# Second attention: exponentials per head out of PSUM, shares divided before they are turned, no matmuls with ones

## What is computed

```python
q = (x @ Wq + bq).reshape(B, N, NUM_HEADS, HEAD_DIM)
k = (y @ Wk + bk).reshape(B, M, NUM_HEADS, HEAD_DIM)
v = (y @ Wv + bv).reshape(B, M, NUM_HEADS, HEAD_DIM)
scale = 1.0 / np.sqrt(HEAD_DIM)
scores = jnp.einsum('bnhd,bmhd->bhnm', q, k) * scale
attn = jax.nn.softmax(scores, axis=-1)
out = jnp.einsum('bhnm,bmhd->bnhd', attn, v).reshape(B, N, IMAGE_DIM)
h = jax.nn.relu(out @ W1 + b1)
return h @ W2 + b2
```

## Time and profile before

| | |
|---|---|
| median of three runs | 781.83 us (780.53 to 781.97) |
| span of the profiled execution | 779.1 us |
| busy: PE, PEld | 651.9 us (84%), 451.2 us (58%) |
| busy: DVE, ACT, POOL | 369.5 us (47%), 221.6 us (28%), 181.0 us (23%) |
| chain that ended last, by engine | PE 56%, issue 16%, DVE 8%, DMA 8%, ACT 5% |
| mean granted clock of PE | 0.937 of full speed |

### The profile page before, as it was taken

The page is one execution under the profiler, slowest core; times in us unless marked ns, Lnnn a source line. Parts: engine busy times, 40 slices in busy tenths (PEclk is TensorE's granted clock), DMA queues, the critical chain, the costliest instruction groups (busy, mean ns, idle before and its releaser), DMA issues.

```text
span 779.1 us, 10605 instructions
## 1 busy us (share of the span) xinstructions
PE 651.9 (84%) x3506; PEld 451.2 (58%) x3507; DVE 369.5 (47%) x925; ACT 221.6 (28%) x361; POOL 181.0 (23%) x151
## 2 busy tenths in 40 slices
PE   4968689998799988999978973198999989898993
PEld 3746457686477863768746752145555555555552
DVE  4443649638486384685536675622232222222221
ACT  1241254431455224454124410021221212121220
POOL 2100223002330013120022100413333333334332
PEclk9987799999999998999988995589999999999998
DMA  9900100002000011000070202012222222222222
GB/s 351 407 21 1 54 1 1 2 21 94 14 0 0 20 54 54 0 0 0 0 261 36 82 0 58 7 29 41 41 41 41 40 42 34 43 35 43 36 35 26
DMA packets 20756, 40.27 MB, mean 52 GB/s; under 512 B 3872, under 2 KB 17440, under 8 KB 19456
## 3 DMA queue, kind: packets, MB, share of 16 engines
q1 hardware_dynamic: 8736, 25.16, 8.6%
q0 software_dynamic: 7488, 10.39, 8.2%
q10 hardware_dynamic: 4512, 4.46, 1.7%
HBM read 30.37 MB, written 9.64 MB: 51 GB/s over the span
## 4 chain that ended last, share of the span: by engine, by line
PE 56%; issue 16%; DVE 8%; DMA 8%; ACT 5%; POOL 3%; DVEq 3%; POOLq 1%; ACTq 0%
PE ps L617 33%; PE ps L948 11%; PE ps L621 8%; DMA keep<-normed,row_in 6%; PE ps L963 4%; POOL var_xh L300 1%; ACT ring L482 1%; DVE mx L1127 1%; DMA out_x<-OT,row_out 1%; DVEq L1040 1%; ACT keep L586 1%; DVE ring L1131 1%; POOL ring L357 1%; DVE rc L1137 1%; DVE XH L1008 1%
## 5 line engine op out<-in xcount | busy, mean ns | idle before, releaser
L948 PE MATMUL ps<-experts,keep 128*128 x312 | 144.7, 607 | 8.1 <-ACT keep L586 7.8
L1404 DVE SCALAR_TENSOR_TENSOR keep<-keep,row_w,ps 128x512 f32<-128x512 f32 x39 | 29.2, 749 | 151.9 <-ACT keep L590 151.9
L948 PEld LDWEIGHTS ps<-experts,keep 128*128 128x128 f32 x312 | 56.9, 192 | 70.1 <-issue 69.7
L374 POOL DMA_INDIRECT out_x<-OT,row_out x39 | 61.8, 1584 | 147.9 <-DVE row_out L1412 86.6
L963 PE MATMUL ps<-experts,keep 128*128 x312 | 73.9, 380 | 2.0 <-DVE keep L1408 2.0
L300 POOL TENSOR_TENSOR var_xh<-var_xh,minus_half 128x4 f32<-128x4 f32 x16 | 16.9, 1059 | 250.4 <-DVE var_xh L1003 250.4
L617 PE MATMUL ps<-experts,keep 128*128 128x256 f32 (+1 forms) x184 | 70.1, 533 | 5.9 <-DVE experts L1067 2.8
L963 PEld LDWEIGHTS ps<-experts,keep 128*128 128x128 f32 x312 | 59.1, 190 | 26.2 <-issue 20.1
L617 PE MATMUL ps<-ring,V 128*32 128x128 f32 x512 | 64.3, 279 | 1.5 <-DVE OT L1139 1.5
L1127 DVE TENSOR_REDUCE mx<-ps 128x8 f32<-128x1024 f32 x32 | 39.1, 1220 | 53.8 <-PE ps L617 53.8
L617 PE MATMUL ps<-ring,keep 128*32 128x128 f32 x512 | 63.5, 273 | 0.0
(11 more groups left out here) (209 smaller groups left out, 942.9 us busy)
## 6 DMA issues: line engine op xcount, KB each, us to landing
experts<-in_experts SPq DMA_DIRECT2D x8, 1536.0 KB, 16.6
keep<-in_keep SPq DMA_DIRECT2D x1, 3075.0 KB, 19.1
ring<-in_fold SPq DMA_DIRECT2D x1, 2112.0 KB, 11.2
experts<-in_x SPq DMA_DIRECT2D x4, 512.0 KB, 3.5
experts<-in_ctxT SPq DMA_DIRECT2D x4, 512.0 KB, 4.1
out_x<-X ACTq DMA_DIRECT2D x4, 512.0 KB, 3.1
normed<-XH ACTq DMA_DIRECT2D x4, 512.0 KB, 4.0
experts<-in_ctx SPq DMA_DIRECT2D x4, 384.0 KB, 3.4
```

Source lines behind the costliest of these rows:

```text
L374: pool.indirect_dma_start(out=out_d, out_offset=bass.IndirectOffsetOnAxis(ap=row_out[u][:, 0:1], axis=0), in_=YO[u], in_offset=None, compu ...
L948: ins = pe.matmul(ps[:, 2 * u + g, :], XIT[u][:, k, :], experts[:, bass.ds(at + (2 * k + g) * INTER, INTER)], start=(k == 0), stop=(k == K ...
L1404: dve.scalar_tensor_tensor(HA[u], HA[u], row_w[u][:, 0:1], ps[:, 2 * u + 1, :], ALU.mult, ALU.mult).then_inc(act_ok, 1)
```

## The change

The softmax of the second attention is rearranged. `most1` takes the place of `shift`: DVE still finds the largest score of each head, and then makes of it minus the largest times the scale (128 x 8 values), and no longer subtracts. `exp1` becomes eight instructions, one for each head: ACT reads the 128 scores of the head from PSUM, with the bias of the head, writes `PP`, and accumulates their sum into one column of `den`. `share1` on DVE takes the reciprocal of the eight sums and multiplies all 1024 exponentials by it. Transposes, their copy and `attend1` follow; `attend1` has no matmuls with ones, and goes over the stripes first and over the two halves of the heads second, so that matmuls in a row write different stripes. `keep1` copies the result from PSUM to `OT`. The streams are ordered anew around it, and the scores' banks are given back by the exponentials instead of by the subtraction.

```diff
-            def exp1(n, u):
-                act.wait_ge(s["sub"], UNITS * n + u + 1)
-                act.activation(PP[u % 2], PP[u % 2], ACT.Exp, scale=float(HD) ** -0.5).then_inc(s["exp"], 1)
+            def exp1(n, u, at=3):
+                act.wait_ge(s["mx"], UNITS * n + u + 1)
+                if u >= 2:
+                    act.wait_ge(s["pt_ps"], UNITS * n + u - 1)
+                for h in range(HT8):
+                    ins = act.activation(PP[u % 2][:, h, :], bank(at + h // HT4)[:, h % HT4 * S:(h % HT4 + 1) * S], ACT.Exp,
+                                         bias=mx[u % 2][:, h:h + 1], scale=float(HD) ** -0.5, accum_out=den[u % 2][:, h:h + 1])
+                ins.then_inc(s["exp"], 1)
...
             query1(LAST)
             value1(LAST)
+            exp1(LAST, 0)
             for u in range(UNITS):
-                exp1(LAST, u)
+                if u + 1 < UNITS:
+                    exp1(LAST, u + 1, 0 if u % 2 == 0 else 3)
                 probs1_turned(LAST, u)
...
                 pe.wait_ge(s["kb"], UNITS * n + u + 1)
                 if u >= ahead:
-                    pe.wait_ge(s["sub"], UNITS * n + u + 1 - ahead)
+                    pe.wait_ge(s["exp"], UNITS * n + u + 1 - ahead)
...
             def turn_probs1(n, u):
-                pe.wait_ge(s["exp"], UNITS * n + u + 1)
+                pe.wait_ge(s["norm"], UNITS * n + u + 1)
...
-                for st in range(4):
-                    out = ps[32 * st:32 * st + 32, attend_bank(u), :]
-                    mm(out[:, 0:S], [(V1[:, bb, o, 32 * (4 * t + st):32 * (4 * t + st) + 32], PQ[u % 2][:, 2 * st + o, :]) for o in range(2)])
-                    ins = mm(out[:, S:2 * S], [(kept("ones_half", 2)[:, o, :], PQ[u % 2][:, 2 * st + o, :]) for o in range(2)])
+                for o in range(2):
+                    for st in range(4):
+                        ins = pe.matmul(ps[32 * st:32 * st + 32, attend_bank(u), 0:S], V1[:, bb, o, 32 * (4 * t + st):32 * (4 * t + st) + 32],
+                                        PQ[u % 2][:, 2 * st + o, :], start=(o == 0), stop=(o == 1))
...
-            def shift(n, u, at=3):
-                sc = ps[:, at:at + 2, :].rearrange("p t (h n) -> p (t h) n", h=4)
+            def most1(n, u, at=3):
                 dve.wait_ge(s["sc_ps"], UNITS * n + u + 1)
-                dve.tensor_reduce(mx[u % 2][:, :], sc, AXX, ALU.max)
-                settle()
-                if u >= 2:
-                    dve.wait_ge(s["pt_ps"], UNITS * n + u - 1)
-                dve.tensor_tensor(PP[u % 2], sc, mx[u % 2][:, :].unsqueeze(2).broadcast_to([P, HT8, S]), ALU.subtract).then_inc(s["sub"], 1)
-
-            def divide(n, u):
+                dve.tensor_reduce(mx[u % 2][:, :], ps[:, at:at + 2, :].rearrange("p t (h n) -> p (t h) n", h=4), AXX, ALU.max)
+                settle()
+                dve.tensor_scalar(mx[u % 2][:, :], mx[u % 2][:, :], -float(HD) ** -0.5, None, ALU.mult).then_inc(s["mx"], 1)
+
+            def share1(n, u):
+                dve.wait_ge(s["exp"], UNITS * n + u + 1)
+                dve.reciprocal(den[u % 2][:, :], den[u % 2][:, :])
+                settle()
+                dve.tensor_tensor(PP[u % 2], PP[u % 2], den[u % 2][:, :].unsqueeze(2).broadcast_to([P, HT8, S]), ALU.mult).then_inc(s["norm"], 1)
+
+            def keep1(n, u):
                 bb, t = u // 2, u % 2
                 dve.wait_ge(s["ot_ps"], UNITS * n + u + 1)
-                o = attend_bank(u)
-                dve.reciprocal(rc[u % 2][:, :], bank(o)[:, S:2 * S])
-                settle()
-                dve.tensor_tensor(OT[:, t, bb * S:(bb + 1) * S], bank(o)[:, 0:S], rc[u % 2][:, :], ALU.mult).then_inc(s["ot"], 1)
+                dve.tensor_copy(OT[:, t, bb * S:(bb + 1) * S], bank(attend_bank(u))[:, 0:S]).then_inc(s["ot"], 1)
...
-                divide(n, 3)
-                shift(n, 6)
-                divide(n, 4)
-                shift(n, 7)
+                for u in (4, 5, 6):
+                    share1(n, u)
+                    most1(n, u + 1)
+                    keep1(n, u - 1)
                 top(n + 1)
...
+            most1(LAST, 0)
             for u in range(UNITS):
-                shift(LAST, u, 0 if u % 2 else 3)
-                if u >= 2:
-                    divide(LAST, u - 2)
-            divide(LAST, UNITS - 2)
-            divide(LAST, UNITS - 1)
+                if u + 1 < UNITS:
+                    most1(LAST, u + 1, 0 if u % 2 == 0 else 3)
+                share1(LAST, u)
+                if u:
+                    keep1(LAST, u - 1)
+            keep1(LAST, UNITS - 1)
```

More of the change, by code:

```diff
@@ L163, in build @@
         mx = [sb(f"mx{n}", [P, HT8]) for n in range(2)]
-        rc = [sb(f"rc{n}", [P, P]) for n in range(2)]
+        den = [sb(f"den{n}", [P, HT8]) for n in range(2)]
         gl = sb("gl", [P, B, NE])
@@ L209, in build @@
                  "xh3 xb xT3_ps xT3 k_ps k v1_ps v1 q1_ps q1 f_ps f y_ps xh4 xT4_ps xT4 gl_ps gl "
-                 "kb sc_ps sub exp pt_ps pt ot_ps ot")
+                 "kb sc_ps mx exp norm pt_ps pt ot_ps ot")
         names += "".join(f" var_{m} rs_{m}" for m in norms)
@@ L541, in _ @@
                 query(n + 1)
+                exp1(n, 1)
                 probs1_turned(n, 0)
-                exp1(n, 1)
                 exp_scores(n + 1)
+                exp1(n, 2)
                 probs1_turned(n, 1)
@@ L548, in _ @@
                 for u in (2, 3, 4):
-                    exp1(n, u)
+                    exp1(n, u + 1)
                     probs1_turned(n, u)
                 rows2_turned(n + 1)
-                exp1(n, 5)
+                exp1(n, 6)
                 probs1_turned(n, 5)
                 hidden(n + 1)
-                exp1(n, 6)
+                exp1(n, 7)
                 probs1_turned(n, 6)
-                exp1(n, 7)
                 exp_logits(n + 1)
@@ L866, in _ @@
                 score1(n, 2)
+                attend1(n, 0)
                 turn_probs1(n, 1)
-                attend1(n, 0)
                 turn_probs(n + 1)
                 score1(n, 3)
+                attend1(n, 1)
                 attend(n + 1)
                 turn_probs1(n, 2)
-                attend1(n, 1)
                 score1(n, 4)
+                attend1(n, 2)
                 turn_probs1(n, 3)
-                attend1(n, 2)
                 score1(n, 5)
+                attend1(n, 3)
                 turn_probs1(n, 4)
                 turn_x2(n + 1)
-                attend1(n, 3)
                 score1(n, 6)
+                attend1(n, 4)
                 turn_probs1(n, 5)
-                attend1(n, 4)
                 hidden(n + 1)
                 score1(n, 7)
+                attend1(n, 5)
+                turn_probs1(n, 6)
                 logits(n + 1)
-                turn_probs1(n, 6)
-                attend1(n, 5)
+                attend1(n, 6)
                 turn_probs1(n, 7)
-                attend1(n, 6)
                 attend1(n, 7)
@@ L1271, in _ @@
                 norm_in(n + 1)
-                shift(n, 0)
-                shift(n, 1)
+                most1(n, 0)
+                share1(n, 0)
+                most1(n, 1)
                 most(n + 1)
-                shift(n, 2)
-                divide(n, 0)
+                share1(n, 1)
+                most1(n, 2)
+                keep1(n, 0)
                 over_sum(n + 1)
-                shift(n, 3)
+                share1(n, 2)
+                most1(n, 3)
+                keep1(n, 1)
                 add_attention(n + 1)
-                divide(n, 1)
                 gather_stats("xh2")
-                shift(n, 4)
+                share1(n, 3)
+                most1(n, 4)
+                keep1(n, 2)
                 norm(n + 1, X0, XH0, D, "xh2")
-                divide(n, 2)
-                shift(n, 5)
-                divide(n, 3)
-                shift(n, 6)
-                divide(n, 4)
-                shift(n, 7)
+                for u in (4, 5, 6):
+                    share1(n, u)
+                    most1(n, u + 1)
+                    keep1(n, u - 1)
                 top(n + 1)
-                divide(n, 5)
-                divide(n, 6)
-                divide(n, 7)
+                share1(n, 7)
+                keep1(n, 6)
+                keep1(n, 7)
                 shares(n + 1)
```

## The result

The kernel after takes 822.1 us in the median (819.5 to 826.8), the kernel before 781.87: a ratio of 1.0525 [1.049, 1.056], slower by 40 us.

The account below looks back on a forecast made before the run. PE bounds the kernel before; after the change, rings of waits and a falling clock. 1.8 + 9.3 + 8.7 + 10.5 = 30.3 us on the 779.1 us span gives 809.4, as median 812; range 790 to 829.

Parts of the forecast that it names:

- rival B: PE stays at half clock for nearly all of the attention: 50 us slower, 832 us; chance 0.13.
- rival D: `attend1` gains nothing by going abreast (2.4 us): 10 us more, 822; chance 0.56 together with the forecast.
- Behind the loop, the ring: Last attention: waits through PE, DVE and ACT make 6.15 us a unit instead of 4.47, +9.3 us.
- `attend1` at 0.95 us: Matmuls of `attend1` run two abreast, 0.95 us instead of 2.4; four abreast would be 0.5.
- The clock behind the loop, "half of it", 8.7: Last attention: half clock for five units and the tail costs 17.5 us; half counted, 8.7.
- The clock in the loop, 10.5: Loop trips: clock falls at the trip's end (3 us) and in the middle (0.5), 10.5 us in three trips.
- The loop's ring, +0.6 a trip: Loop: one pair of score banks makes 5.9 us a unit, a trip 0.6 us longer, 1.8 us in three.
- 0.17 for the small multiply: In `most1` on DVE, the small multiply behind the largest scores takes 0.17 us of 1.47.
- In the loop PE was at 1.00 throughout: Kernel before, loop: PE's granted clock was 1.00 throughout; falls were expected there after the change.
- Exponentials, 2.88 us a unit: ACT: eight per-head exponentials at 0.345 us each with the sum's read, 2.88 us with the last one's end.
- A (the clock holds, 793): Clock holds at 2.4 GHz where it did; only the two rings remain, 11 us slower, 793; chance 0.22.
- C (faster): Loop is bound by work, not its ring: 41 us instead of 52.1, in full 758 us; chance 0.09.

Follow-up runs that it names:

- after_warm: The kernel after plus matmuls nothing reads, added where PE idles behind the loop and in its trips; 795.7 us, 1.0174 of before.
- before_order: The kernel before with only the order of `attend1`'s matmuls changed, stripes in the inner loop, all sixteen kept; 755.6 us, 0.9668 of before.
- after_nosums: The kernel after with its eight exponentials a unit no longer accumulating their sums, shares left undivided; 804.5 us, 1.0307 of before.

## Why the prediction was right, and where it was off

The direction and the mechanism were right: PE has less to do, the rings take the place of its work, and the clock follows. The sum was short by 10 us (812 for 822), between the forecast and rival B. That 822 is also the number of rival D is chance, since what D supposes did not happen.

- **Behind the loop, the ring.** Forecast 6.15 us a unit at full clock and +9.3. after_warm shows 5.70, links in the order forecast, and +8.2 (49.7 against 41.6). The 0.45 less is mostly `attend1`. By the forecast's own scale a shorter `attend1` should have brought the +9.3 to some +6.5; the small multiply, held for 1.8 us in one unit (below), makes most of the difference.
- **`attend1` at 0.95 us.** Mis-sized: 0.57 at full clock, the fourfold case. The forecast took two abreast from the earlier trace rows; but no four matmuls in a row wrote four stripes there, so the rows could not show more. D (no gain) is refuted.
- **The clock behind the loop, "half of it", 8.7.** Measured 12.0. The whole attention at half would have been 17.5, and the stretch stood at 0.68: some two thirds of it, not half.
- **The clock in the loop, 10.5.** Measured 12.4 between the profiled executions of after and after_warm; 14.4 if all that the medians leave is put there. The falls come where they were expected, `hidden1` at 8.39 among them, and once more in mid-trip: scores of units 3 and 5 both take 2.08 in trip 2.
- **The loop's ring, +0.6 a trip.** This failed. Measured as the forecast did, from the first exponential to `hidden1`, it is 52.1 us in trips 1 and 2 of before (55.1 in trip 3, with its pause and half clock), 58.2 to 58.5 in after, and with the clock mostly held, in after_warm, 56.4, 55.7 and 55.7. So the ring costs 3.6 us a trip and more. The term that failed is "0.17 for the small multiply", taken without a look at what GpSimd does beside it: twice a trip, in units 0 and 5, it takes 1.7 to 2.1 us, and the second of these lies in the stretch of the forecast. In trip 2 of after_warm the starts of scores from unit 2 on are 5.7, 6.7, 8.1, 7.4 and 6.0 us apart, not 5.9. The 7.4 holds the multiply. The 8.1 is `add_attention`, which puts the product of unit 3 back (its exponentials end at 230.0, its reciprocal starts at 232.28) by 2.4 us in all where the forecast had 1.4. In the 6.7 the scores still run at half clock (2.08). Taking the multiply out (after_min) gives 3.1 to 3.9 us a stage, 15.5 in all, with the drain and the clock that go with it.
- **"In the loop PE was at 1.00 throughout".** That stretch is the first trip. The third trip of before fell to half clock (0.55 from 302.8 to 309.4 us), so a fall in the loop needs none of this change.
- **Exponentials, 2.88 us a unit.** Right (2.75 to 2.92). That the sums are the dear part of them, 27 us in the order of before, stood in no term, since the forecast priced the form as a whole.
- **A (the clock holds, 793).** after_warm nearly makes this case: 795.7. Its condition was wrong. Its size fits in part by luck: the ring of the loop is six times the 0.6 us a trip that it had, and the slow starts of trips 2 and 3 of before hide some of that.
- **C (faster).** The work that goes from PE is real, but 44 us of it (2.4 to 1.01 in 32 units) come from the order of the matmuls alone: 26 us reach the end in before_order. The forecast put the two edits of `attend1` in one term, and so did not see that the gain needs none of the rest, and that removing the ones brings 5.8.

From before_order to after the ladder reads: cutting the exponential +9.6, sums +27.4, out of PSUM without the subtraction +4.1, `share1` +31.2, ones -5.8. Each step is the difference of two medians, and with other neighbours it would be another number: after_nosums gives 17.6 for the sums. The small steps (+4.1, -5.8, +9.6) are near what the pause at the start of a trip can move. No run parts the 31.2 of `share1` into ring and clock.

## What to carry to other kernels

Follow the unit once round through all engines before moving work off the busiest one; where each engine waits for the one before it, the longest way round sets the pace, and the idle time then lowers the clock as well. Try the edits of one change apart: the one that only reordered instructions was worth 26 us, and the others together cost 66. A cut-up instruction is paid in latency on that way round, so price it with its accumulator reads, and price small vector instructions beside what GpSimd runs at the time.

## What the runs showed of the hardware

- Four matmuls of 128 x 128 by 32 columns that write four different stripes run abreast, each set of four starting within 0.02 us: 16 records in 0.46 to 0.57 us. In stripe-by-stripe order 32 records took 2.4 us, stripes first 1.01.
- An accumulated sum is not free on ACT: eight exponentials of 128 from SBUF take 1.70 us without and about 2.35 with sums, from PSUM 2.18 and 2.8 to 2.9. From one start to the next it is 0.20 and 0.29 us out of SBUF, 0.25 and 0.34 out of PSUM.
- A DVE instruction on 128 x 8 values, with one or with two inputs in SBUF, takes 0.17 us alone and up to 2.11 beside a GpSimd `tensor_tensor` of 512 or 1024 columns (1.0 to 2.3 us), and ends within 0.03 us of it. Reductions out of PSUM were not held (1.22 us, also where they began beside one). Nor was the product of `share1` where it began beside GpSimd's instruction on 128 x 4 values (1.23 us at 233.26 in after).
- The clock of PE moves within a stage: in after it is 0.98 and 0.50 in the two stretches

```profile
230.00:238.00 8.00, 2.93 (x30) 1.56 (x28) 6.97 (x19) 3.66 (x18) 2.06 (x2) 0.98 0.00 0
...
454.00:466.00 12.00, 7.43 (x52) 4.36 (x53) 4.70 (x6) 5.72 (x23) 2.99 (x2) 0.50 0.00 0
```

In the first PE has been busy for 2.9 of 8 us and still has the full clock; the scores behind it (238.96) run at half. In the second it works 7.4 of 12 us, and stays at half throughout.
